# Attention of a graph kernel: float32 row tiles for the scores, denominators from a matmul of ones, another order of work

## The reference

```python
x = _layernorm(x + _L0_gnn_ref(...))   # graph convolutions and LSTMs
x = _layernorm(x + _L1_gnn_ref(x, L1_gnn_W, adj))
x = _layernorm(x + _L2_gnn_ref(x, adj, ...))
x = _layernorm(x + _L3_gnn_ref(x, ...))

def _L1_gnn_ref(h, W, adj):
    qkv = (h @ W).reshape(Bn, Nn, 3, H, HEAD_DIM).transpose(2, 0, 3, 1, 4)
    q, k, v = (qkv[0], qkv[1], qkv[2])
    mask = jnp.where(adj == 0, -jnp.inf, 0.0)
    scores = jnp.einsum('bhid,bhjd->bhij', q, k) / np.sqrt(HEAD_DIM) + mask
    attn = jax.nn.softmax(scores, axis=-1)
    out = jnp.einsum('bhij,bhjd->bhid', attn, v)
    return out.transpose(0, 2, 1, 3).reshape(Bn, Nn, OUT_DIM)

def _L2_gnn_ref(features, A, W1, b1, g1, be1, W2, b2, g2, be2):
    agg = jnp.einsum('nm,bmd->bnd', A_hat, features)
    h = jax.nn.relu(_batchnorm(agg.reshape(-1, d) @ W1.T + b1, g1, be1))
    ...
```

## Time and profile before

| | us |
|---|---|
| three runs | 1688.45, 1684.99, 1684.6 |
| median | 1684.99 |
| profiled execution, its own time | 1689.47 |
| span of the profiled execution | 1687.7 |

### The profile page before, as it was taken

One profiled execution on the slowest core, in us unless ns is written; L12 is line 12 of the kernel. 1 busy time (PEld: TensorE's weight loads), 2 busy tenths in 40 slices (PEclk: granted clock), 3 DMA queues, 4 the chain that ended last, 5 costly groups with the idle time before them and its releaser, 6 DMA issues.

```text
span 1687.7 us, 28097 instructions
## 1 busy us (share of the span) xinstructions
PE 1514.9 (90%) x9014; PEld 1208.4 (72%) x9076; DVE 1263.0 (75%) x2989; ACT 1042.9 (62%) x1984; POOL 407.1 (24%) x641
## 2 busy tenths in 40 slices
PE   3999999899989989995699999999999879899997
PEld 3888888787888888895477767677777645555554
DVE  3578767677776777777688888888888745577775
ACT  2666576566656666664466666666666436557776
POOL 2122212112121221221233233323333300023332
PEclk9999999999999999998799999999999979989999
DMA  3000000000000000000000000000000000022221
GB/s 95 1 1 24 15 1 13 14 13 14 1 26 13 1 13 14 13 1 15 1 20 14 19 12 19 19 12 19 12 19 12 19 19 0 0 70 87 87 87 57
DMA packets 19519, 37.62 MB, mean 22 GB/s; under 512 B 3313, under 2 KB 4849, under 8 KB 19313
## 3 DMA queue, kind: packets, MB, share of 16 engines
q1 hardware_dynamic: 18576, 34.49, 6.4%
q10 hardware_dynamic: 864, 2.11, 0.3%
HBM read 19.81 MB, written 16.78 MB: 22 GB/s over the span
## 4 chain that ended last, share of the span: by engine, by line
PE 61%; DVE 18%; ACT 12%; issue 5%; POOL 2%; DMA 1%; ACTq 0%; DVEq 0%; POOLq 0%
PE banks L391 14%; PE banks L393 13%; PE banks L392 13%; PE banks L1497 5%; PE banks L1504 5%; ACT early_scratch L796 4%; PE banks L1464 3%; DVE x_all L506 3%; ACT attention_scratch L750 2%; ACT attention_rounded L750 2%; PE banks L1414 2%; DVE early_scratch L985 2%; PE banks L1424 2%; DVE consts L464 1%; DVE attention_rounded L1035 1%
## 5 line engine op out<-in xcount | busy, mean ns | idle before, releaser
L391 PE MATMUL banks<-early_rounded 128*128 128x128 f32 (+3 forms) x1424 | 458.4, 322 | 64.9 <-DVE early_rounded L990 31.1
L392 PE MATMUL banks<-early_rounded 128*128 128x128 f32 (+3 forms) x1424 | 454.8, 319 | 0.0
L393 PE MATMUL banks<-early_rounded 128*128 128x128 f32 (+3 forms) x1424 | 454.4, 319 | 0.0
L796 ACT ACTIVATE early_scratch<-banks,consts 128x256 f32<-128x256 f32 (+2 forms) x624 | 311.7, 565 | 133.4 <-PE banks L393 119.3
L391 PEld LDWEIGHTS banks<-early_rounded 128*128 128x128 f32 x1424 | 280.3, 197 | 90.3 <-issue 42.0
L392 PEld LDWEIGHTS banks<-early_rounded 128*128 128x128 f32 x1424 | 280.1, 197 | 14.7
L393 PEld LDWEIGHTS banks<-early_rounded 128*128 128x128 f32 x1424 | 280.2, 197 | 14.0
L660 POOL CAST early_rounded<-early_scratch 128x512 fp32r<-128x512 f32 (+2 forms) x160 | 93.5, 594 | 555.7 <-DVE early_scratch L985 555.7
L750 ACT ACTIVATE attention_rounded<-banks 32x512 fp32r<-32x512 f32 (+1 forms) x160 | 94.4, 590 | 100.3 <-PE banks L1376 69.3
L803 ACT ACTIVATE early_scratch<-early_scratch 128x256 f32<-128x256 f32 (+2 forms) x176 | 87.2, 517 | 71.8 <-DVE early_scratch L976 60.9
L985 DVE TENSOR_TENSOR early_scratch<-early_scratch 128x256 f32<-128x256 f32 (+2 forms) x176 | 96.3, 559 | 42.5 <-ACT early_scratch L803 40.2
(11 more groups left out here) (173 smaller groups left out, 3110.6 us busy)
## 6 DMA issues: line engine op xcount, KB each, us to landing
early_scratch<-in_x_dram SPq DMA_DIRECT2D x16, 512.0 KB, 3.5
x_away<-attention_scratch SPq DMA_DIRECT2D x32, 256.0 KB, 2.0
late_scratch<-x_away SPq DMA_DIRECT2D x32, 256.0 KB, 2.7
out_dram<-late_scratch SPq DMA_DIRECT2D x32, 256.0 KB, 2.0
x_all<-in_WihT_dram ACTq DMA_DIRECT2D x1, 1024.0 KB, 5.5
x_all<-in_WhhT_dram ACTq DMA_DIRECT2D x1, 768.0 KB, 7.2
x_all<-in_Wqkv_dram ACTq DMA_DIRECT2D x1, 192.0 KB, 10.5
kept_scratch<-in_W_dram SPq DMA_DIRECT2D x1, 192.0 KB, 2.5
```

What stands on the lines that cost most here:

```text
L391: pe.matmul(out, wt[0], mv[0], start=start, stop=False)
L392: pe.matmul(out, wt[1], mv[0], start=False, stop=False)
L393: return pe.matmul(out, wt[0], mv[1], start=False, stop=stop)
L796: nc.scalar.activation(gate_f[lane][gate][:, 0:cols], bank(bank_set("lstm", n, unit), gate)[:, 0:cols], ACT.Tanh if gate == G else ACT.Sig ...
```

## The change

Keys and queries stay in float32, one copy of 512 columns each. A score becomes float32 matmuls of 32 rows: head h's 32 features lie on partitions 32h to 32h + 31 and use that row tile of the array. All sixteen of a group (four graphs, four heads) go in one step, `scores`, head h into bank h, behind four matmuls of the mask. `soft` and `exp` then work on two graphs at a time, 1024 columns. The values are copied by ScalarE into 32 columns a head without ones; `attend` makes four matmuls with the values and four with a matrix of ones, the head's output and its denominator, into column tiles of 32 of bank 7. `divide` takes a reciprocal of 256 columns and multiplies before the transposes back, of which four remain (`back`). The add of x moves from GpSimd to VectorE, the norm from VectorE to ScalarE, as an activation with scale and bias, for which GpSimd works out one more product. Transposed probabilities and values use bank 6 alone. Orders and latenesses are new on all engines; `bank_free` gives way to waits written out in each step. The product for hat moves ahead of the loop, and the memsets of ones and zeros go.

```diff
                 if what == "keys":
                     act.wait_ge(k_sums, g + 1)
-                    for h in range(HEADS):
-                        copy(key_block(kd_r[place][0], h), by_batch(banks[h * DH:(h + 1) * DH, 4, :], GB))\
-                            .then_inc(k_hi, 1)
+                    wait_if(act, scores, g)
+                    copy(k_f, banks[:, 4, :]).then_inc(k_kept, 1)
...
+                if what == "norm":
+                    act.wait_ge(shift2, g + 1)
...
+                    for b in range(GB):
+                        ins = nc.scalar.activation(x2_f[:, b * P:(b + 1) * P], y_f[:, b * P:(b + 1) * P], ACT.Identity,
+                                                   bias=shift_cols[:, b:b + 1], scale=rstd[:, b:b + 1])
...
-            groups(act, [("turned", 0, 2), ("exp", 2, 3), ("probT", 0, 3), ("keys", 0, 2), ("probT", 1, 3), ("probT", 2, 3), ("exp", 3, 3), ("queries", 0, 2), ("probT", 3, 3), ("round", 0, 4), ("attended", 0, 3), ("exp", 0, 2), ("exp", 1, 2), ("aggregated", 0, 4)], do, pairs=3)
+            groups(act, [("keys", 0, 1), ("queries", 0, 1), ("exp", 0, 2), ("values", 0, 1), ("turned", 0, 0), ("probT", 0, 2),
+                         ("probT", 1, 2), ("exp", 1, 2), ("probT", 2, 2), ("aggregated", 0, 4), ("probT", 3, 2),
+                         ("norm", 0, 3), ("round", 0, 3)], do, pairs=3)
...
                 if what == "divide":
+                    dve.wait_ge(attended, g * GB + 2 * part + 2)
+                    wait_if(dve, att_turned, g)
+                    nc.vector.reciprocal(dens[part], banks[:, 7, 2 * P:4 * P]).then_inc(inverted, 1)
+                    dve.wait_ge(inverted, g * 2 + part + 1)
+                    nc.vector.tensor_tensor(attT[:, part * 2 * P:(part + 1) * 2 * P], banks[:, 7, 0:2 * P],
+                                            dens[part], ALU.mult).then_inc(divided, 1)
+                if what == "add":
                     dve.wait_ge(att_turned, g + 1)
...
+                    nc.vector.tensor_tensor(y_f, banks[:, 7, :], xcols(g), ALU.add).then_inc(y_sums, 1)
...
-            groups(dve, [("queries", 0, 1), ("norm", 0, 3), ("soft", 0, 1), ("soft", 1, 1), ("stats", 1, 4), ("soft", 2, 1), ("agg_low", 0, 3), ("divide", 0, 2), ("values", 0, 1), ("turned", 0, 0), ("soft", 3, 1), ("add", 0, 2), ("stats", 0, 3), ("keys", 0, 0)], do, pairs=3)
+            groups(dve, [("divide", 1, 3), ("soft", 0, 2), ("add", 0, 3), ("soft", 1, 2), ("stats", 0, 5), ("turned", 0, 0),
+                         ("divide", 0, 2), ("agg_low", 0, 4), ("stats", 1, 5)], do, pairs=3)
...
+                if what == "scores":
+                    wait_if(pe, shifted, g * 2)
+                    for h in range(HEADS):
+                        pe.matmul(banks[:, h, :], ident_bf[:, :], mask[:, :], start=True, stop=False)
+                    pe.wait_ge(k_kept, g + 1)
+                    pe.wait_ge(q_kept, g + 1)
+                    for b in range(GB):
+                        for h in range(HEADS):
+                            rows, cols = slice(h * DH, (h + 1) * DH), slice(b * P, (b + 1) * P)
+                            ins = pe.matmul(banks[:, h, cols], q_f[rows, cols], k_f[rows, cols], start=False,
+                                            stop=b == GB - 1)
+                    ins.then_inc(scores, 1)
...
                 if what == "attend":
                     if part == 0:
+                        wait_if(pe, y_sums, g)
+                    if part == 2:
+                        pe.wait_ge(divided, g * 2 + 1)
                     pe.wait_ge(probT_kept, g * GB + part + 1)
+                    at = (part % 2) * P
                     for h in range(HEADS):
+                        rows, of = slice(h * DH, (h + 1) * DH), (part * HEADS + h) * DH
+                        pe.matmul(banks[rows, 7, at:at + P], vals[place][:, of:of + DH],
+                                  probT[part][:, h * P:(h + 1) * P], start=True, stop=True)
+                    for h in range(HEADS):
+                        rows = slice(h * DH, (h + 1) * DH)
+                        ins = pe.matmul(banks[rows, 7, 2 * P + at:3 * P + at], ones_sq[:, 0:DH],
+                                        probT[part][:, h * P:(h + 1) * P], start=True, stop=True)
...
                 if what == "aggregate":
                     pe.wait_ge(x2_lo, g + 1)
+                    pe.wait_ge(xT_lo, upto(g + 5))
+                    wait_if(pe, agg_lo, g)
...
-            ATTENTION = [("score", 1, 1), ("first", 1, 4), ("score", 2, 1), ("aggregate", 0, 3), ("attended", 0, 2), ("values", 0, 1), ("turn", 0, 0), ("probT", 0, 1), ("score", 3, 1), ("keys", 0, 0), ("first", 0, 3), ("attend", 0, 1), ("probT", 1, 1), ("probT", 2, 1), ("queries", 0, 0), ("attend", 1, 1), ("probT", 3, 1), ("attend", 2, 1), ("attend", 3, 1), ("score", 0, 0)]
+            groups(pe, [("scores", 0, 2), ("back", 0, 3), ("keys", 0, 1), ("queries", 0, 1), ("values", 0, 1),
+                        ("turn", 0, 0), ("probT", 0, 2), ("first", 0, 5), ("probT", 1, 2), ("aggregate", 0, 4),
+                        ("attend", 0, 2), ("attend", 1, 2), ("probT", 2, 2), ("first", 1, 5), ("probT", 3, 2),
+                        ("attend", 2, 2), ("attend", 3, 2)], do, pairs=3)
...
+            groups(pool, [("copy", 0, 0), ("rstd", 0, 3), ("x2_low", 0, 3)], do, pairs=3)
```

More of the change, by code:

```diff
@@ L1347, in _, with upto @@
                 pe.wait_ge(x1_kept[lane], units_of(lane))
-            ATTENTION = [("score", 1, 1), ("first", 1, 4), ("score", 2, 1), ("aggregate", 0, 3), ("attended", 0, 2), ("values", 0, 1), ("turn", 0, 0), ("probT", 0, 1), ("score", 3, 1), ("keys", 0, 0), ("first", 0, 3), ("attend", 0, 1), ("probT", 1, 1), ("probT", 2, 1), ("queries", 0, 0), ("attend", 1, 1), ("probT", 3, 1), ("attend", 2, 1), ("attend", 3, 1), ("score", 0, 0)]
-            BANK = {"turn": 4, "keys": 4, "aggregate": 4, "queries": 5, "values": 5, "first": 5}
-            LEFT = {"turn": xT_lo, "keys": k_lo, "aggregate": agg_lo, "queries": q_lo, "values": v_kept,
-                    "first": bn1_done}
-            def bank_free(what, part, g):
-                at = [v[0:2] for v in ATTENTION].index((what, part))
-                behind = ATTENTION[at][2]
-                for _ in range(8 * len(ATTENTION)):
-                    at -= 1
-                    if at < 0:
-                        at, behind = at + len(ATTENTION), behind - 1
-                    user, half, late = ATTENTION[at]
-                    if BANK.get(user) != BANK[what]:
-                        continue
-                    before = g + (behind - late)
-                    if isinstance(before, int) and not 0 <= before < GROUPS:
-                        continue
-                    pe.wait_ge(LEFT[user], before * 2 + (half + 1) if user == "first" else before + 1)
-                    return
+            pe.wait_ge(hat_work_done, 5)
+            pe.wait_ge(ones_made, 1)
+            pe.matmul(banks[:, 0, 0:P], ones_sq, diag, start=True, stop=True).then_inc(hat_product, 1)
+            def upto(g):
+                return min(g, GROUPS) if isinstance(g, int) else g
             def do(what, part, g, place):
@@ L1373, in do @@
                     pe.wait_ge(xg_copied, g + 1)
-                    bank_free(what, part, g)
+                    wait_if(pe, k_kept, g)
                     for b in range(GB):
@@ L1410, in do @@
-                if what == "probT":
-                    pe.wait_ge(exps, g * GB + part + 1)
-                    wait_if(pe, probT_kept, g * GB + part - 1)
+                if what == "scores":
+                    if isinstance(g, int) and g == 0:
+                        pe.wait_ge(hat_turned, 1)
+                    wait_if(pe, shifted, g * 2)
[9 more added lines that the diff above has]
+                    ins.then_inc(scores, 1)
```

208 lines of the change are left out of this document (73 added, 135 removed).

## The result

The changed kernel takes 1695.8 us at the median (1693.86 to 1699.16), against 1684.8 of the kernel before: a ratio of 1.006, with a 95% interval of 1.004 to 1.0081. It is slower by 0.6% where 1% faster was forecast. The profiled execution took 1696.28 (span 1694.5).

What follows compares the result with a forecast made beforehand. In the attention loop TensorE and VectorE were nearly full; new waits tying engines together would set the group. 31 steps (497 us) plus 33.5 make 530.5 against 547.5; with the start, -17.5 gives 1668 us at the median, range 1648 to 1732.

Steps and rivals of the forecast that it cites:

- The sum of 16.25 us a group: attention loop: one group laid out in order across the engines takes 16.25 us, 0.25 less than now.
- rival 3: attention loop: waits lower TensorE's clock in one group of four, 3 us each, 23 in all; 1691 us, chance 0.12.
- the wait ahead of the aggregate: TensorE, each group: stands 1.8 us before the aggregate until VectorE has done 'turned'.
- its allowance of 0.2: added to the group's layout, because the old orders laid out alike gave 16.3 where the trace has 16.5.
- Row tiles: scores on TensorE: 32 records take 1.0 us plus 0.25 for the way in and out; bounds 3.5 and 0.87.
- An attend of 16 records: attends on TensorE, four column tiles: 0.49 us taken; 0.44 if four run at a time, 0.87 if two.
- rivals 1 and 2: 1: tiled records handed out too slowly, 1727 us, chance 0.13; 2: row tiles don't run together, 1745 us, chance 0.10.
- The 0.027 a record: TensorE: densest tiled records in the trace, 16 in 0.44 us, possibly a limit of issue.
- The way in and out: TensorE: going into tiles and out again costs 0.24 us, shared by neighbouring attends; 0.25 taken for the row tiles.
- rival 4: TensorE: the way in and out of tiles is free where the queue is full; -0.5 a group, 1652 us, chance 0.10.
- The reciprocal of 256 columns: VectorE's division: 0.42 us taken, 1.9 if priced by column; both ends hide beside other work.
- Ends: attention stage: first scores at about 816 instead of 816.6; last scores to last statistics 33.5 us.

Runs made afterwards that it cites:

- warm: the changed kernel with six more float32 matmuls on TensorE in front of the transposes of probT 1, inside the wait ahead of the aggregate; 1668.77 us.
- warm_third: the changed kernel with two more float32 matmuls in front of the transposes of probT 1, instead of six; 1666.69 us.
- after: the changed kernel itself, as profiled, against the kernel before; 1695.8 us at the median, ratio 1.006.
- turned_early: the changed kernel with 'turned' ahead of 'stats 0' in VectorE's order, nothing else; 1650.28 us, ratio 0.9789.

## Why the prediction was wrong, by its own steps

**The step that failed** is the clock. The sum of 16.25 us a group takes every row at full clock and has no term for a lower one; that stood in rival 3 alone, with a fall in one group of four and a chance of 0.12. The runs show a fall in 22 of 26 groups at 1.4 us each, 17.28 us instead of 15.89, and the loop takes 517.7 us where 497 were forecast. The mechanism of rival 3 was right: I saw the wait ahead of the aggregate (1.8 forecast, 1.34 measured) and that TensorE would do little in that stretch (1.6 of 4.2 us forecast; 1.97 of 3.35 measured just ahead of the aggregate), and its sign, a clock row below 1.00, came (0.90 in the groups with a fall). Its chance, its count and its price were wrong. That its 1691 lies near 1695.8 is luck, because two factors are off in opposite directions: the price, 3 us, because only the attends 0 and 1 and probT 2 lie in the slow stretch while the aggregate is through before it; the count, because no row stood behind one in four. The rows at hand show 20 us with little work, and no row of the kernel before shows a short wait in a busy loop that brings the clock down: from 860 to 1300 us its granted clock is 1.00, and its waits there, such as the 0.32 of the earlier trace rows, are short.

**The sum without the clock was near.** warm, warm_third and the fall-free groups of after give 15.8 to 16.0 us a group, where 16.25 was forecast with its allowance of 0.2, and the two runs take 1668.8 and 1666.7 us in all, where 1668 was forecast. That the totals agree to 1 us is in part luck: in the trace of warm the middle groups are 0.37 shorter than forecast, but the first three steps last 18.8, 15.0 and 15.7 us instead of 13.6, 13.6 and 16.25, and the end of the stage 38.2 instead of 33.5.

**Terms.** Row tiles: the 32 records go from 1112.47 to 0.90 later (1.17 less the 0.27 of one, the median in the profile) and the last step, 1.0 as taken; that is 3.5 times as fast as one after another. By the estimate from the Trainium skill, "TensorE: Matmul & The Clock Gate", Part 3, whose speedup of 3.07 is for 512 columns, it would have been 1.14; these 128 columns did better. The 1.0 lies between that and the 0.87 of four at a time, because the way in is part of it: behind the first set, sets of four start 0.11 apart by the trace's records, the step of one full matmul. An attend of 16 records takes 0.51 at full clock, half of warm's 1.02 for two, ways in and out included (taken 0.49 without them), so four column tiles run together as well. With these two, rivals 1 and 2 fall: the records are not handed out too slowly, and the tiles do overlap. The 0.027 a record that spoke for rival 1 was a mean over sixteen, and no limit: by its records the two matmuls of a pair of column tiles start 0.006 us apart already in the trace of before (1105.318 and 1105.324), and the four of a set in after 0.006 to 0.007. Attends 0 and 1 together were taken at 1.2 with the ways; the step from attend 3 to the masks is 0.58 (1110.90 to 1111.48), where 0.75 was taken. The way in and out is cheaper than taken in full queues, a part of rival 4. The reciprocal of 256 columns takes 1.76, near its upper bound of 1.9 and far from the 0.42 taken, and VectorE is busy 13.0 us a group instead of about 11; that the reciprocal costs nothing held, to 0.06 us a group at full clock in warm. The 1024-wide maxima take 1.21 and 1.22 (taken 1.2). The norm on ScalarE takes 1.65 and ScalarE stands 2.33 before the next keys: nothing, as forecast.

**Ends.** Against the forecast of -17.5 the spans differ by +6.8, 24.3 more. The steps of the loop give 21 of these (517.7 against 497) and the end 4.6 (from the last group's first masks at 1330.6 to the end of the last statistics at 1368.7, 38.1 against 33.5); the start gives 3.1 back (812.9 instead of 816); 2.2 more come behind the loop, where the code is the same (325.8 against 323.6 from the end of the last statistics to the end of the span). The cause of the last stays open.

## What to carry to other kernels

When a change takes work off the matrix engine and ties it to another engine's chain, price the new wait twice: as lost time, and as a cause of a lower clock for the work behind it. Where TensorE must wait, put into the wait work that is ready (here the attends: 62 us less with an order alone) before shortening other things. And look at the granted clock group by group: a mean of 0.9 over the loop was a fall in most groups at the same place.

## What was not expected of the hardware

A wait of 1.33 to 1.34 us, once in a group of 16 to 17 us in which TensorE is otherwise busy, was followed by a stretch at 1.2 GHz in 22 of 26 groups; at 0.73 (turned_early) and 0.84 us (warm_third) none was. With the same wait and 1.3 us more matmuls elsewhere in the group it was 3 of 26, and with a wait of 1.44 to 1.54 us 16 of 26, which the wait alone doesn't explain.

Two sizes of float32 reciprocal show a price by column: 8 columns take 0.18 us, 256 columns 1.76, while a multiplication of 256 takes 0.42. That is some 6.4 ns a column, an estimate from these two ((1.76 - 0.18) / 248).
